# A finer interleaving of two streams of work in the first sum of a graph network kernel

## The reference

```python
h = relu(layernorm(x)); x = x + segment_sum(edge_weight * (sigmoid(h @ Wg + b) * (h @ W))[dst], src)
h = relu(layernorm(x)); x = x + segment_sum(h[src], dst) @ W1.T + b1
h = relu(layernorm(x)); x = x + L2(h)      # messages from h[src] and h[dst], summed by dst, then an update
h = relu(layernorm(x)); x = x + relu(batchnorm(L3(h)))   # two segment sums, nodes -> hyperedges -> nodes
```

## Time and profile before

| | us |
|---|---|
| median of 3 runs | 2613.72 (2612.69 to 2618.68) |
| profiled execution, its own time | 2625.16 |
| its span in the trace | 2623.4 |
| busy: PE / DVE / ACT | 2342.7 / 1601.8 / 1235.6 |
| mean granted clock of TensorE | 0.966 |

### The profile page before, as it was taken

How to read it: one execution, slowest core, us unless ns; L and a number is a source line. 1 busy time by engine, 2 the same in 40 slices (tenths; PEclk the granted TensorE clock), 3 DMA queues, 4 the chain that set the end, 5 groups by cost and what they waited for, 6 DMA issues and landing times. The chain is left out here.

```text
span 2623.4 us, 71483 instructions
## 1 busy us (share of the span) xinstructions
PE 2342.7 (89%) x27976; PEld 2004.2 (76%) x27976; DVE 1601.8 (61%) x3701; ACT 1235.6 (47%) x2695; POOL 38.0 (1%) x46
## 2 busy tenths in 40 slices
PE   2689999999989998999938999899998999999996
PEld 2468787778777777777837888788887888887884
DVE  6689999999999998999962333234333222121224
ACT  2578787778777777777732222222222000011113
POOL 3100000000000000000000000000000000000000
PEclk9889999999999999999979999999998999999996
DMA  6279999999999999999999999899997999999994
GB/s 188 65 143 204 217 212 216 204 204 208 219 181 207 202 203 195 204 203 199 202 230 233 283 284 282 228 261 258 253 257 202 290 289 290 272 256 248 266 268 114
DMA packets 1595771, 586.11 MB, mean 223 GB/s; under 512 B 951206, under 2 KB 1592234, under 8 KB 1595351
## 3 DMA queue, kind: packets, MB, share of 16 engines
q1 hardware_dynamic: 1592219, 574.02, 99.5%
q0 software_dynamic: 1600, 4.92, 0.6%
q10 hardware_dynamic: 1660, 3.20, 0.5%
HBM read 255.26 MB, written 89.20 MB: 131 GB/s over the span
## 5 line engine op out<-in xcount | busy, mean ns | idle before, releaser
L1159 ACT CAST stage<-ps 128x784 f16<-128x784 f32 x784 | 654.4, 835 | 97.2 <-DMA counts_by_source<-stage 61.9
L617 PE MATMUL ps<-Ha,a_tiles 128*128 128x258 f16 x4802 | 548.2, 274 | 46.3 <-ACT Ha L1206 38.9
L617 PEld LDWEIGHTS ps<-Ha,a_tiles 128*128 128x128 f16 x4802 | 470.0, 98 | 116.8 <-ACT Ha L1206 39.1
L570 PE MATMUL ps<-hot_c,hot_r 128*128 128x98 f16 x3136 | 508.7, 212 | 11.6 <-DVE hot_c L868 5.9
L571 PE MATMUL ps<-hot_c,hot_r 128*128 128x98 f16 x3136 | 502.8, 210 | 0.0
L572 PE MATMUL ps<-hot_c,hot_r 128*128 128x98 f16 x3136 | 501.5, 210 | 0.0
L1144 ACT CAST stage<-ps 128x392 f16<-128x392 f32 x784 | 397.3, 507 | 169.2 <-PE ps L553 169.2
L545 PE MATMUL ps<-g_in,wt 128*128 128x128 f16 x2401 | 430.7, 222 | 44.2 <-DVE X L880 33.0
L546 PE MATMUL ps<-g_in,wt 128*128 128x128 f16 x2401 | 427.8, 221 | 0.0
L547 PE MATMUL ps<-g_in,wt 128*128 128x128 f16 x2401 | 427.6, 221 | 0.0
L880 DVE SCALAR_TENSOR_TENSOR X<-ps,X 128x512 f32<-128x512 f32 (+1 forms) x637 | 390.4, 649 | 15.5 <-PE ps L547 15.5
(11 more groups left out here) (199 smaller groups left out, 2084.0 us busy)
## 6 DMA issues: line engine op xcount, KB each, us to landing
a_tiles<-counts_by_source SPq DMA_DIRECT2D x147, 1600.0 KB, 9.2
counts_by_source<-stage SPq DMA_DIRECT2D x49, 1600.0 KB, 8.0
gated_parts<-G SPq DMA_DIRECT2D x7, 448.0 KB, 3.0
g_in<-gated_parts SPq DMA_DIRECT2D x98, 32.0 KB, 2.9
out_x<-X SPq DMA_DIRECT2D x6, 512.0 KB
edge_table<-tab SPq DMA_DIRECT2D x1, 2448.0 KB, 9.8
wt<-stage SPq DMA_TRANSPOSE x98, 10.8
dst_run<-in_dst SPq DMA_DIRECT2D x1, 612.4 KB
```

Source lines behind the costliest of these rows:

```text
L570: mm(into(0), rows_, codes(0), start=v == 0, stop=True, skip_group_check=True)
L617: last = mm(ps[:, c % 2, 0:PARTS], a_slot(ph, c, i), moving[:, i], start=i == 0, stop=i == TILES - 1)
L1159: a.copy(stage[:, b, 0:2, 0:TILES, u * SET_COLS:(u + 1) * SET_COLS], of).then_inc(s("hi_done"), 1)
```

## The change

The same instructions are issued with the same operands; the order in the build changes on two engines. TensorE takes one unit, one group, one unit, one group where it took two units and two groups. VectorE takes codes, addition, rows, addition, weights where it took codes, rows, weights, addition, addition. ScalarE and SP keep their programs. No wait is added or removed; each stays in front of the instruction that it guards, except that the wait for the transposed weights (`wt_in`, `g_loaded`) now stands after unit 0 of a tile instead of after unit 1. In the tail, the groups of the last two tiles keep their order.

```diff
-def summed_at(h):
-    return range(2 * h, min(2 * h + 2, FOURS))
...
-                def sums(t, b, n, h):
-
-                    if h == 0:
+                def sums(t, b, n, h, half):
+
+                    if h == 0 and half == 0:
                         pe.wait_ge(s(f"wt_in{b}"), n * 32)
                         pe.wait_ge(s(f"g_loaded{b}"), n * 32)
-                    for g in summed_at(h):
-                        sum_four(t, b, g)
+                    if 2 * h + half < FOURS:
+                        sum_four(t, b, 2 * h + half)
 
                 def build(j, k, c):
                     for h in range(TILE_HOTS):
                         pe.wait_ge(s("hot_ready"), j * TILE_HOTS + (h + 1))
-                        half_windows(j, c % 2, c, 2 * h)
-                        half_windows(j, c % 2, c, 2 * h + 1)
-                        if later(j, 2):
-                            sums(j - 2, c % 2, k * (SLOTS // 2) + c // 2, h)
+                        for half in range(2):
+                            half_windows(j, c % 2, c, 2 * h + half)
+                            if later(j, 2):
+                                sums(j - 2, c % 2, k * (SLOTS // 2) + c // 2, h, half)
...
-                def hots(j, h):
+                def hots(j, h, add):
...
                     v.tensor_tensor(hot_c[:, b, :, 0], iota_c[:].rearrange("p i d a -> p (i d) a").unsqueeze(1).to_broadcast([P, PAIRS, WCOLS, 2]), key(1, WCOLS), ALU.is_equal).then_inc(s("hot_codes"), 1)
+                    add(0)
                     v.tensor_tensor(hot_r[:, b], iota_r[:].unsqueeze(1).to_broadcast([P, PAIRS, P, 2]), key(0, P), ALU.is_equal)
+                    add(1)
                     dve.wait_ge(s("hot_codes"), hot + 1)
                     v.tensor_tensor(hot_c[:, b, :, 1:1 + WEIGHTS], hot_c[:, b, :, 0].unsqueeze(2).to_broadcast([P, PAIRS, WEIGHTS, WCOLS, 2]),
...
                     for h in range(TILE_HOTS):
-                        hots(j, h)
-
                         t, tb, hh = (j - 2, b, h - 2) if h >= 2 else (j - 3, 1 - b, h + TILE_HOTS - 2)
-                        if not isinstance(t, int) or t >= 0:
-                            for g in summed_at(hh):
-                                add_four(t, tb, g)
+
+                        def add(half):
+                            if (not isinstance(t, int) or t >= 0) and 2 * hh + half < FOURS:
+                                add_four(t, tb, 2 * hh + half)
+
+                        hots(j, h, add)
```

More of the change, by code:

```diff
@@ L599, in layers @@
                         for h in range(TILE_HOTS):
-                            sums(t, t % 2, t // 2 + 1, h)
+                            for half in range(2):
+                                sums(t, t % 2, t // 2 + 1, h, half)
                 for ph in (1, 2, 3, 4):
@@ L903, in layers @@
                     for h in range(TILE_HOTS - 2, TILE_HOTS):
-                        for g in summed_at(h):
+                        for g in range(2 * h, min(2 * h + 2, FOURS)):
                             add_four(TILES - 3, 0, g)
```

## The result

The changed kernel takes 2626.24 us (median of 7 runs, 2621.25 to 2631.41) where the kernel before took 2618.47 in the same comparison: ratio 1.0037, 95% interval 1.0022 to 1.0052, so 8 to 10 us slower. A second series gave 1.0027 (1.0010 to 1.0045), 7 us. How far such intervals can be trusted shows in a copy of the kernel before, measured against itself: 0.9974 (0.9950 to 0.9999). The change is slower by about 0.3%, with the two series agreeing in sign; its size is known to a few us at best.

What follows compares the result with a forecast made beforehand. VectorE's pace plus stalls from the DMA chain were taken to bound the build; 12 us from the longer two-tile loop and 2 from the clock, on 2613.7, gave 2628 us, own range 2619 to 2638, over all 2600 to 2646.

Steps and rivals of the forecast that it cites:

- What bounds the kernel: Build: VectorE's pace, 23.08 us a tile, plus 1.22 us of stall a tile, from SP's chain of two transposes and store.
- VectorE's order costs nothing by itself: VectorE's hots with two additions: reordered instructions still take 3.16 us; upper bound 94 us if new seams did not overlap.
- Rival 3: Slower by more: the loop codes, addition, group, unit, codes breaks at disturbances, 2645 us; seam cost has the same sign; chance 0.13.
- The tight loop in the middle hots holds with 0.3 us to spare: Hots 4 to 7: the second unit is ready at 2.84 us, VectorE asks for it at 3.16; nothing lost.
- S to the codes of hot 3, +0.31 us: Tile's beginning, from its first high copy's start: a group now stands before unit 3, making these codes 0.31 us later.
- Codes of hot 7 to E, +0.21: Tile's end: later weights of hot 7 make the last high copy end 0.21 us later, counted from hot 7's codes.
- Tiles with slack in the loop don't escape: Tiles not held by the DMA chain: unit 3 ready 5.14 us after hot 0, asked for at 4.99; about 0.2 lost.
- W + D grows by 0.52 us per two tiles, 12 us: First to last high copy, plus chain until the buffer's next first copy: 0.52 us longer, 23 times from tile 3 on.
- D: 0: SP's chain from last high copy's end to the buffer's next first copy: unchanged, between -2.1 and +0.3 us.
- Rival 1: Faster: evenly spaced copies shorten the chain of transposes and store, 19 us against the +12, 2607 us; chance 0.22.
- Clock, 2 us: Four tiles with TensorE's clock slow after long stalls: one more group ahead of the needed unit, about 0.5 us each.
- The signs: Expected in the changed profile: among others, tiles of 24.6 us on average, codes waiting 50 to 60 us instead of 39.

## Why the prediction was right, and where it was not

The time was forecast 14 us up, and is 8 to 10 up; direction and rough size hold. The steps behind it:

- *What bounds the kernel*: held. VectorE's 23.08 us a tile, stalled by the DMA chain at hot 3. With one transpose less the stalls are gone and the tile takes 23.11.
- *VectorE's order costs nothing by itself*: held for the seams: 3.16 us a hot, and the new seams overlap like the old. The upper bound of 94 us has no case here. Rival 3 sets the old seams against a rule of the Trainium skill, "VectorE: DVE Perf Modes", "The DRAIN you can't avoid". The same section adds that an operation which isn't held starts earlier, so the overlap of 0.08 us in the earlier trace rows doesn't contradict it.
- *The tight loop in the middle hots holds with 0.3 us to spare*: held; the codes of hots 4 to 7 wait in no ordinary tile. The slack in VectorE's order is needed: with TensorE's order alone it fails, at 320 us.
- *S to the codes of hot 3, +0.31 us*: measured 3.43 where it was 3.14, in tiles where the stored counts hold S (3.56 and 3.28 in the loop). *Codes of hot 7 to E, +0.21*: measured 6.15 where it was 5.95; in the loop 6.22. Both sizes are right. Whether they cost anything isn't settled: the kernel with VectorE's new order alone keeps the late E and is as fast as before, but it also has fewer long chains, and the one with hot 0 in pairs keeps both terms and is 0.24% slower.
- *"Tiles with slack in the loop don't escape ... such a tile loses about 0.2"*: this is the step that failed by its size. It checked the codes of hot 3, three units and three groups after `hot_ready`, and not those of hot 2. With the same numbers: unit 0.74, group 0.66 and unit 0.94 make 2.34 us, and VectorE asks after 1.96 - 0.13 = 1.83. It is 0.51 late; 0.52 was measured unrolled, 0.72 in the loop, in every tile, 33 us in all where nothing else stalls. The lateness at hot 3 is real as well: it shows as 0.31 us once the group of hot 0 is moved, and is hidden behind the wait of hot 2 otherwise.
- *W + D grows by 0.52 us per two tiles, 12 us*: failed as the term of the time. A tile must satisfy both the loop and VectorE's own path with its wait, and the later of the two counts, not their sum. In the new order VectorE's path is 23.61 to 23.82 us; (W + D) / 2 for a loop tile, with W = 3.56 + 4 x 3.16 + 6.22 = 22.4 and D = 24.9, is 23.7. In the old order the same sum is 23.5 (W = 21.9, D = 25.1), above VectorE's 23.11.
- *D: 0*: missed, within the stated bounds. The mean is 0.48 us shorter in one pair of profiles and 0.46 in the other, just short of the 0.5 us that was to prove the forecast wrong, and the intervals over 26 us went from 8 or 9 a profile to 1 or 2. Rival 1 named this and priced it at 19 us; by my estimate 23 pairs of tiles at 0.47 us are 11, about as much as the 12 us of the term above. Fewer long chains come with VectorE's order alone too (2 over 26 us, mean 25.06). Why, no run shows.
- *Clock, 2 us*: the second stalls at hot 4 did not grow in the changed kernel's traces (none in the first, one of 0.51 us in the second), since the long stalls before them became rare. This term was not there.

- *The signs*: tiles of 24.6 us on average and 50 to 60 us of waiting codes did not come: it was 24.24 us (24.16 in the second profile) against 24.30, and 37.3 us, though 52 times. They belonged to stalls at hot 3; the waits came at hot 2.

So a forecast of 14 came from two terms that were right in size and are not shown to make the cost, and it left out two larger effects of opposite sign: VectorE's wait at hot 2, some 30 us, and the stalls on the DMA chain that go in exchange. That the sum came out near is in part luck. What the runs show is that TensorE's order makes the loss, and that the whole change costs 33 us where the chain does not bind. How 33 us of added waits and the stalls they replace make 8 us rather than 2 or 15 isn't settled: the profiled executions of one pair differ by 2.4 us and of the other by 3.3, the timed runs by 8 and 7, and over the 44 tiles the changed kernel is the shorter one in both pairs, by 2.6 and 0.6 us.

## What to carry to other kernels

When an order is made finer, the place to check is not the typical step but the one where the partner engine has least to do, and there every consumer along the path from the first one on: a piece set between two others delays what is asked for soonest. A wait that is new in the trace costs only what no stall of another loop took in its place; to know its full price, take the other loop away in both versions and compare.

## What the runs showed of the hardware

The DMA engines were fuller than expected. Two transposes of about 8 us in the queue each and a store of 1600 KB take a median of 24.9 to 25.1 us from the last copy to the next first copy, whichever comes first; with the store first, a 32 KB load behind it took 3.55 us in the queue in place of 0.34. VectorE's overlap of 0.08 us between two instructions is lost when the second one has to wait, so that a wait of 0.43 us costs 0.52. At each turn of the loop over 12 tiles VectorE stood still for 3.9 to 5.4 us, waiting for nothing that the profile shows, and the two tiles there took 5.5 to 10 us more than two plain ones, in the four profiles of the two kernels. With one transpose a tile less the two tiles took 4.5 to 6.4 us more; what holds them was not tried. And a kernel measured against its own copy, in 6 and 15 runs, came out at 0.9974, its interval just short of one.
